# Second attention: GPSIMD takes one in four of head 1's row-sum tiles below the diagonal

## What is computed

```
scores = einsum('bhtd,bhsd->bhts', Qf, Kf) * 32 ** -0.5
scores = where(causal, scores, finfo.min)
attn = softmax(scores, axis=-1)
out = einsum('bhts,bhsd->bhtd', attn, V)      # 16 heads, 2048 tokens
```

## Time and profile before

| | |
|---|---|
| Median of 3 runs | 2696.15 us (2688.54 to 2734.21) |
| The profiled execution's own time | 2693.72 us |
| Its span, first to last instruction | 2692.0 us |
| Mean granted TensorE clock | 0.944 |
| Second attention | from 1972.5 us (first pass 1 product) to about 2602 us |
| First exponential, last block maximum | 2003.1 us, 2555.2 us |

### The profile page before, as it was taken

How to read it: one execution, slowest core, us unless ns; L and a number is a source line. 1 busy time by engine, 2 the same in 40 slices (tenths; PEclk the granted TensorE clock), 3 DMA queues, 4 the chain that set the end, 5 groups by cost and what they waited for, 6 DMA issues and landing times. The chain is left out here.

```text
span 2692.0 us, 42224 instructions
## 1 busy us (share of the span) xinstructions
PE 2394.0 (89%) x16394; PEld 1498.7 (56%) x16394; DVE 1749.8 (65%) x2066; ACT 1249.9 (46%) x2372; POOL 566.8 (21%) x480
## 2 busy tenths in 40 slices
PE   4959999969999999999999869979969999999947
PEld 2748888846555444444444347758745555555515
DVE  3745444555767878888886043422259999999954
ACT  2422222204555767777788522212215655656531
POOL 1110000030000000000000002220036766666650
PEclk8979999977999999999999889989989999999978
DMA  3771000034321211000000020015562222220024
GB/s 123 238 231 48 32 32 31 0 62 85 82 61 38 58 45 30 30 30 21 29 18 15 13 67 1 0 48 116 192 145 47 51 65 65 65 63 10 8 67 144
DMA packets 133182, 168.60 MB, mean 63 GB/s; under 512 B 60736, under 2 KB 70592, under 8 KB 129920
## 3 DMA queue, kind: packets, MB, share of 16 engines
q1 hardware_dynamic: 129536, 153.45, 21.5%
q10 hardware_dynamic: 3456, 12.58, 1.5%
HBM read 114.19 MB, written 51.64 MB: 62 GB/s over the span
## 5 line engine op out<-in xcount | busy, mean ns | idle before, releaser
L710 ACT ACTIVATE a_ex<-a_ps_s 128x512 f32<-128x512 f32 (+3 forms) x1280 | 620.0, 532 | 331.3 <-PE a_ps_s L793 249.3
L913 DVE TENSOR_REDUCE a_mx_part<-a_ps 128x2 f32<-128x1024 f32 (+3 forms) x576 | 584.0, 1043 | 132.2 <-PE a_ps L739 129.7
L1206 ACT ACTIVATE a_ex<-a_ps_s 128x512 f32<-128x512 f32 (+3 forms) x640 | 318.3, 532 | 285.9 <-PE a_ps_s L1267 160.3
L793 PE MATMUL a_ps_s<-a_q,a_k 50*128 50x512 f32 (+3 forms) x1152 | 395.9, 419 | 2.8 <-ACT a_ex L710 2.8
L1181 POOL TENSOR_TENSOR a_acc<-a_acc,a_ex 128x512 f32<-128x512 f32 (+3 forms) x288 | 352.0, 1222 | 95.8 <-ACT a_ex L1206 75.0
L739 PE MATMUL a_ps<-a_k,a_q 48*128 48x512 f32 (+3 forms) x1152 | 346.0, 418 | 27.4 <-DVE a_low_q L898 14.8
L837 PE MATMUL a_ps_o<-a_ex,a_v 128*32 128x256 f32 (+1 forms) x5120 | 361.8, 364 | 4.9 <-ACT a_o L680 4.2
L1331 DVE TENSOR_REDUCE a_mx_part<-a_ps 128x2 f32<-128x1024 f32 (+2 forms) x320 | 336.1, 1054 | 32.4 <-PE a_ps L1233 22.8
L793 PEld LDWEIGHTS a_ps_s<-a_q,a_k 50*128 50x128 f32 x1152 | 180.7, 188 | 206.4 <-ACT a_ex L710 144.2
L1230 PE MATMUL a_ps<-a_k,a_q 96*128 96x512 f32 (+3 forms) x640 | 211.6, 397 | 44.1 <-DMA a_q<-q 22.9
L1372 DVE TENSOR_TENSOR a_acc<-a_acc,a_ex 128x512 f32<-128x512 f32 (+3 forms) x288 | 248.8, 864 | 2.3 <-ACT a_ex L1206 0.2
(11 more groups left out here) (218 smaller groups left out, 3898.8 us busy)
## 6 DMA issues: line engine op xcount, KB each, us to landing
a_q<-q SPq DMA_DIRECT2D x192, 64.0 KB, 2.3
a_k<-k SPq DMA_DIRECT2D x24, 512.0 KB, 5.2
a_q<-q SPq DMA_DIRECT2D x24, 512.0 KB, 7.2
q<-p_oh SPq DMA_DIRECT2D x32, 256.0 KB, 2.4
q<-p_ol SPq DMA_DIRECT2D x32, 256.0 KB, 2.6
o<-a_o SPq DMA_DIRECT2D x32, 256.0 KB, 2.2
a_v<-v SPq DMA_DIRECT2D x12, 512.0 KB, 7.6
mlp_raw<-in_wup SPq DMA_DIRECT2D x5, 1024.0 KB, 5.0
```

What stands on the lines that cost most here:

```text
L710: act.activation(ex[unit % NE][:, h % 2, off:CH], ps_s[n % 3][:, off:CH], ACT.Exp, scale=SCALE)\
L793: pe.matmul(ps_s[n % 3][:, off:CH], k_st[r0:r0 + KM, g, t * P:(t + 1) * P], q_st[b % NQ][r0:r0 + KM, h // HALVES, off:CH], start=True, sto ...
L913: dve.tensor_reduce(part[:, 2 * p:2 * p + 2, i - TPC * c, kc], bank[:, :, 0:w], AX.X, ALU.max).then_inc(taken1, 1)
L1206: act.activation(ex[s % NE][:, h, off:CH], ps_s[n % 3][:, off:CH], ACT.Exp, scale=SCALE)\
```

## The change

A list `LENT` marks the steps with t % 4 == 2 and t < 4c: one in chunk 1 (t = 2), two in chunk 2 (t = 2, 6) and three in chunk 3 (t = 2, 6, 10), so 6 in a group and 48 in all. On these steps VectorE does not add head 1's tile. GPSIMD does it right after head 0's add, into a total of its own, `acc_lent`: the first of a chunk (t = 2) is a copy, the others are adds, so 24 copies and 24 adds. In chunks 1 to 3 the sums get a third product, `acc_lent` with the ones, accumulated onto head 1's. The counters' targets are recomputed (`ADDED0`, `ADDED1`). To make room, the flipped maxima no longer have tiles of their own: they use partitions 64 to 71 of the tile `z_sb`, which becomes 128 partitions high, and the flip writes partitions 64 to 71 of its buffer.

More of the change, by code:

```diff
@@ L1092, in put_rows @@
                 for part in range(2):
-                    sp.dma_start(m_d[f, part], rows[b][part][:, :].bitcast(F32)).then_inc(rows_out[b], 16)
+                    sp.dma_start(m_d[f, part], rows[b][part].bitcast(F32)).then_inc(rows_out[b], 16)
                 sp.wait_ge(rows_out[b], 32 * (f // 2 + 1))
@@ L1248, in sums @@
                 pe.wait_ge(taken1, m - 1)
-                pe.wait_ge(added0, s + 1)
-                pe.wait_ge(added1, s + 1)
+                pe.wait_ge(added0, ADDED0[s])
+                pe.wait_ge(added1, ADDED1[s])
+                lent = j % NCH > 0
                 for h in range(HG):
                     mm = pe.matmul(ps_1[m % 2][h * DH:(h + 1) * DH, 0, :], one[:, :], acc[j % 2][h][:, :],
-                                   start=True, stop=True)
+                                   start=True, stop=h == 0 or not lent)
+                if lent:
+                    mm = pe.matmul(ps_1[m % 2][DH:HG * DH, 0, :], one[:, :], acc_lent[j % 2][:, :], start=False, stop=True)
                 mm.then_inc(scores1, 1)
@@ L1347, in take_rows @@
                     dve.wait_ge(rows_out[f % 2], 32 * (f // 2))
-                dve.tensor_copy(high[:, :], bank).then_inc(row_high, 1)
+                dve.tensor_copy(high, bank).then_inc(row_high, 1)
                 dve.wait_ge(row_high, f + 1)
-                dve.tensor_tensor(low[:, :], bank, high[:, :].bitcast(F32), ALU.subtract).then_inc(taken1, 1)
+                dve.tensor_tensor(low, bank, high.bitcast(F32), ALU.subtract).then_inc(taken1, 1)
             def take_sums(n):
@@ L1357, in take_sums @@
                     dve.wait_ge(z_stored[j % 2], 16 * HG * (j // 2))
-                dve.tensor_copy(z_sb[j % 2][:, :], ps_1[m % 2][0:OR, 0, :]).then_inc(taken1, 1)
+                dve.tensor_copy(z_sb[j % 2][0:OR, :], ps_1[m % 2][0:OR, 0, :]).then_inc(taken1, 1)
             def add_ex(s):
@@ L1370, in add_ex @@
                     return
-                dve.wait_ge(added1, s)
+                dve.wait_ge(added1, ADDED1[s - 1])
                 dve.tensor_tensor(total[:, off:CH], total[:, off:CH], tile, ALU.add).then_inc(added1, 1)
```

## The result

The changed kernel takes 2723.73 us (median of 20 runs, 2714.18 to 2743.09), the kernel before 2702.99 us (20 runs, 2683.90 to 2734.21). The ratio is 1.0105, 95% interval 1.0079 to 1.0131: about 28 us slower. The forecast was 2686 us, with a range of 2662 to 2709.

What follows compares the result with a forecast made beforehand. VectorE was taken as the bound until the last maximum, TensorE close behind. A gain of 12.8 us over 7.3 groups less 4.8 in the tail made 8 us off 2693.7, so 2686 us, range 2662 to 2709.

Steps and rivals of the forecast that it cites:

- VectorE's account: Per group, VectorE: 4.9 us of slots freed, less 1.2 for slower other adds and 0.3 for moved rows, 3.4 us.
- the 3.8 that the forecast let TensorE turn into time: Per group, of VectorE's 4.9 us TensorE can use 0.6 in chunk 1, 1.1 in chunk 2, 2.1 in chunk 3.
- the forecast of -1.75: Net gain per group: TensorE's account 2.5 us less 0.75, half of VectorE's 1.5 of costs; 12.8 us over 7.3 groups.
- A lag of one or two steps costs nothing: GPSIMD's queue on lent steps: a late add is covered, since ScalarE reuses a tile only eight steps later.
- Forecast 1.2 us a group by an average of full adds: VectorE's remaining adds wait longer as GPSIMD's work grows: 16% of 7.5 us, between bounds of 0 and 6.9.
- rival C: Lent steps: two back-to-back GPSIMD instructions delay VectorE's next add, 6.9 us a group; full adds about 1.3; 2716 us, 12%.
- 1.3 us a group forecast: Third product, 0.85 us each: free at a group's start, uncovered in chunk 2, half covered in chunk 3.
- Rival D: Group starts: the clock falls to 1.2 GHz, 3 us a fall; falls at all give 2698 to 2700, none takes 8 off; 15%.
- Forecast +4.8 us: Tail: four lent tiles cost 3.5 us and one more last sum about 1.3, all exposed; bounds 2 to 7.
- B: Port shared by VectorE and GPSIMD as the floor: 1.6 us a group more, 12 us, and the tail's 4.8; 2711 us, 8%.
- rival E: Second attention stage: TensorE is the bound outright, so the relief does nothing; 2708 us, 3%.

Runs made afterwards that it cites:

- the relief alone with the clock held: Kernel before, nobody adds head 1's 48 marked tiles, idle products added to TensorE's list at group starts: ratio 0.9887 to the kernel before, copies 73.44 us apart.
- the relief alone: Kernel before, but nobody adds head 1's 48 marked tiles, no idle products: ratio 1.0019 to the kernel before, interval 0.9987 to 1.0050.
- The load alone: Changed kernel, VectorE keeps all adds, GPSIMD adds the marked tiles too, no third product: ratio 1.0129 to the kernel before; with idle products 76.54 us a group.

## Why the prediction was wrong

**What bounds the kernel.** "So VectorE is the bound until the last maximum" was the wrong reading. VectorE was busy 578.3 of 598 us, but its adds have waiting inside their rows (1.035 us in the mean against 0.67), and most of that time proved to be slack. What it is worth to be rid of six adds is 0.85 us a group, shown by the relief alone with the clock held, not 3.4 (VectorE's account) and not the 3.8 that the forecast let TensorE turn into time. The failed step is this one: waits of TensorE for VectorE in a stretch (1.1, at least 2.5) were taken as time that any relief in that stretch can use. It makes 2.95 of the 3.4 us a group that lie between the forecast of -1.75 and the +1.65 at one clock. The waits stood elsewhere than the marked tiles. Of the 9.9 us in the fifth group, 3.1 stand in steps 1 and 2 of the group and 6.2 in the four steps with the sums, and the relief with the clock held left 6.1 of these as they were. The 2.5 us that the earlier trace rows give to chunk 3 were also misread: its stretch runs to 2304 us, past the next group's start, and 0.53 of them belong there. A reading that fits, and was not tested: TensorE and VectorE are two score banks apart, so an add that goes away at t = 2, 6 or 10 makes VectorE early for an entry that TensorE has not yet computed, and the lead is gone at the next one.

**GPSIMD.** "A lag of one or two steps costs nothing" held for ScalarE (its wait for GPSIMD is 2.2 us) and failed for VectorE. The lag reached the narrow adds at the group's start, where TensorE waits for VectorE. Forecast 1.2 us a group by an average of full adds, of which half was to show; measured about 1.8 alone with the clock held (2.3 with the moved rows). The full adds' mean didn't rise, as rival C would have it (1.069, not 1.3). The 256-wide add of chunk 3 did, from 0.42 to 1.25 us; but GPSIMD's lag is not the only way to that, for with the relief alone it took 1.09 at six of the seven starts.

**The parts together.** The whole is 76.0, less than the parts added to 74.3: -0.85, 1.84 and 2.3 make 77.6, and 77.1 when the moved rows are counted once. The steps say where the rest goes. The load alone lengthens steps 7 to 11 of chunk 2 by 1.3 us, where the whole change has 0.1; and in step 5 of chunk 2 the load's 0.56 and the product's 0.79 are 0.79 together. So at one clock load and relief nearly cancel, and the change costs what the third product and the moved rows cost.

**The third product.** 0.85 us each was right (0.86, 0.79), and so was the sum, 1.3 us a group forecast and about 1.3 measured. But the places were wrong, so the sum was luck: the one at the start of a group, which was to cost nothing, cost 0.86, and the one in chunk 3, which was to cost half, cost nothing.

**The clock.** Rival D had the place and the price (2.7 to 3.1 us a fall) and 15%. It was priced as chance, and at a start of the kernel before it looks like chance: two stretches with TensorE equally busy, the first with a fall behind it and the second without.
```profile
2378.00:2381.40 3.40, 2.40 (x17) 1.78 (x15) 3.24 (x7) 1.50 (x5) 0.88 (x2) 1.00 0.00 1
2302.90:2306.30 3.40, 2.39 (x18) 1.36 (x17) 3.37 (x7) 1.36 (x4) 1.74 (x2) 1.00 0.03 5
```
The change made TensorE idle longer there (1.57 busy of 3.40 us), and the fall came at all seven starts. A wait of that depth is not needed, since with the relief alone the clock fell at six starts behind 2.1 to 2.2 us of work in 3.4; nor did it always suffice, since the changed kernel without the third product had one start without a fall behind such a wait. That idle time is needed is shown by the idle products. Why the relief alone brings more falls stays open. Between the changed kernel as it is (78.5) and with the clock held (75.96) lie 2.6 us a group, 18 us; in the kernel before, its three falls cost 6.4.

**The moved rows.** 0.3 us a group forecast, 0.6 as the upper bound; 0.5 measured, in two groups of one profile, too little to show in the total.

**The tail.** Forecast +4.8 us. With the clock held in both, the last group is 64.6 against 63.6 us and the rest after the start of the last exponential 106.5 against 102.8: +4.8. The agreement is partly luck: the idle products do not hold the clock there, and from the last group's start on it was low for 54 us in the one profile and 57 in the other. The 1.57 us of a tail step was also an average over three narrow tiles; the full ones stand 1.69 us apart.

The sum again, at the profiled execution: 7 x 1.65 = 11.5 and the tail's 4.8 are the change with the clock held, 16 us; the clock adds 16 more (18 less the 6 of the falls before, and 4 in the tail), and the earlier stages took 7 off, 25 in all. The runs, where the earlier stages average out, give 28.

**Ranges.** The upper end of 2709 left out B and C, which ended at 2711 and 2716, and no case joined D with a loss of its own, which is what came. At one clock, without the falls, the change costs 16 us, nearest to rival E, which had 14 and 3%.

Open: why the load's cost at the end of chunk 2 goes away with the relief, why the moved rows cost what they do, and what decides over a fall where the same wait has one at some starts and none at others.

## What to carry to other kernels

An engine that is 97% busy in a profile may not be the bound if its rows contain waiting; compare each shape's mean with its shortest, and look at which steps the other engines wait in before you take their waits as time to win. Work handed to a queue that has slack on average can arrive late where that queue's backlog ends; look at which consumer meets it there. And where TensorE idles shortly at a regular place, the clock is part of the price: filling the wait with idle products gave 0.43% (12 us, interval 3 to 20) here, where the relief that the change aims at is worth 7 (8 groups by 0.85).

## What the runs showed of the hardware

A 256-wide VectorE add that started 0.04 us after a GPSIMD add took 1.25 us instead of 0.42. A product of 128x512 by 32 columns, put behind another on the same column strip, lengthened TensorE's list by 0.86 us at 2.4 GHz (1.84 against 0.98 to the next load). In all profiles of this case each fall of the granted clock at a group's start followed a stretch in which TensorE stood partly still, and none came where 17 or 23 idle products of 128 columns filled the wait; 17 cost 0.1 us a group (74.28 against 74.17). A fall at a start cost about 2.7 us in the kernel before (76.91 against 74.17) and 2.6 in the changed one.
